# Audio tower on one core: z turned beside pv, tokenizer units that end at halves of a cycle, and q and k projected behind the experts' first products

## What is computed

```python
h = tok(x)                                        # x: 16 x 512 x 128
h = h + attn(layernorm(h))
h = h + ffn(layernorm(h))

# tok: for patches of 8, 16, 32 rows with half a patch as stride
y = einsum('bnk,dk->bnd', patches, W) + b + pos + scale_emb[i]   # 127 + 63 + 31 = 221 rows a batch
# attn: 8 heads of 16, 221 x 221 scores
attn = softmax(q @ k.T / sqrt(16)); out = (attn @ v) @ w_agg.T + b_agg
# ffn: the first 1024 tokens, 8 experts, each token goes to 2 of them
h1 = gelu(xg @ w1[e]); y = h1 @ w2[e]; out[token] += weight * y
```

## Time and profile before

| | us |
|---|---|
| median of 3 timed runs | 293.25 |
| lowest, highest | 283.29, 294.13 |
| the profiled execution | 283.87 |
| its span, first to last instruction | 281.8 |
| TensorE busy in it | 244.3 |
| VectorE, ScalarE, GpSimd busy | 191.2, 140.2, 124.8 |
| mean granted clock of TensorE | 0.973 |

### The profile page before, as it was taken

The page is one execution under the profiler, slowest core; times in us unless marked ns, Lnnn a source line. Parts: engine busy times, 40 slices in busy tenths (PEclk is TensorE's granted clock), DMA queues, the critical chain, the costliest instruction groups (busy, mean ns, idle before and its releaser), DMA issues.

```text
span 281.8 us, 6982 instructions
## 1 busy us (share of the span) xinstructions
PE 244.3 (87%) x2711; PEld 202.4 (72%) x2711; DVE 191.2 (68%) x420; ACT 140.2 (50%) x220; POOL 124.8 (44%) x177
## 2 busy tenths in 40 slices
PE   8999986997997879998896598989898989897894
PEld 8799776765675667776666486868686868685673
DVE  2994765857687758697855337676767676758644
ACT  4860310633323142524355256767676767676460
POOL 6000120111236345647474144868686858664421
PEclk9999999898899999999999689999999999999998
DMA  6999030305437282743332312626363625343422
GB/s 220 416 386 464 9 87 11 87 12 125 139 72 218 50 220 57 206 121 96 89 85 63 73 37 45 127 48 124 50 123 51 125 48 114 49 92 44 101 19 41
DMA packets 29903, 32.00 MB, mean 114 GB/s; under 512 B 3798, under 2 KB 26150, under 8 KB 29840
## 3 DMA queue, kind: packets, MB, share of 16 engines
q1 hardware_dynamic: 25374, 28.39, 35.5%
q0 software_dynamic: 4080, 2.59, 7.2%
q10 hardware_dynamic: 418, 0.58, 0.6%
HBM read 16.24 MB, written 5.95 MB: 79 GB/s over the span
## 4 chain that ended last, share of the span: by engine, by line
PE 66%; DVE 18%; ACT 5%; issue 4%; DMA 3%; SPq 1%; POOL 1%; DVEq 0%; POOLq 0%; ACTq 0%
PE s_ps L1268 13%; PE e_ps L1194 13%; DVE nmax L968 10%; PE e_ps L1462 8%; PE s_ps L1194 8%; PE m_ps L1253 4%; PE m_ps L1447 4%; ACT probs L663 3%; PE e_ps L1447 3%; DMA x_raw<-x 2%; PE m_ps L1410 2%; ACT hidT L715 1%; PE m_ps L1259 1%; PE m_ps L1381 1%; PE m_ps L1260 1%
## 5 line engine op out<-in xcount | busy, mean ns | idle before, releaser
L968 DVE TENSOR_REDUCE nmax<-s_ps 104x4 fp32r<-104x884 f32 (+1 forms) x60 | 61.9, 1073 | 29.2 <-PE s_ps L1268 29.1
L663 ACT ACTIVATE probs<-s_ps 104x888 f32<-104x888 f32 (+1 forms) x60 | 51.3, 907 | 40.3 <-PE s_ps L1268 39.8
L562 POOL DMA_INDIRECT out<-y_sb,idx_u x23 | 36.4, 1582 | 39.6 <-DMA out<-y_sb,idx_u 20.8
L1268 PE MATMUL s_ps<-pair_a 32*104 32x222 f32 (+1 forms) x504 | 34.9, 311 | 15.1 <-DVE nmax L968 10.0
L1268 PEld LDWEIGHTS s_ps<-pair_a 32*104 32x104 f32 (+1 forms) x504 | 21.3, 172 | 30.7 <-DVE nmax L968 15.7
L500 POOL TENSOR_TENSOR var_eps<-mv,eps_t 128x2 f32<-128x2 f32 x16 | 7.0, 437 | 66.4 <-DVE mv L933 66.3
L533 POOL DMA_INDIRECT z_slots<-z,slot_u x20 | 21.3, 1067 | 20.4 <-PE s_ps L1268 16.3
L1462 PE MATMUL e_ps<-w_now,hidT 128*128 128x128 f32 x184 | 25.6, 292 | 2.8 <-DVE zsT L1070 2.7
L1462 PEld LDWEIGHTS e_ps<-w_now,hidT 128*128 128x128 f32 x184 | 23.4, 204 | 4.3 <-issue 4.0
L1381 PE MATMUL m_ps<-probs,v_aug 104*32 104x221 f32 (+1 forms) x480 | 25.8, 353 | 0.0
L1194 PE MATMUL e_ps<-x_hi,w_hi 128*128 128x248 f32 (+3 forms) x88 | 20.1, 361 | 4.4 <-DVE hT L825 4.4
(11 more groups left out here) (163 smaller groups left out, 515.5 us busy)
## 6 DMA issues: line engine op xcount, KB each, us to landing
pair_a<-qk SPq DMA_DIRECT2D x64, 111.0 KB
w_sb<-w SPq DMA_DIRECT2D x8, 512.0 KB
pair_b<-qk SPq DMA_DIRECT2D x32, 111.0 KB
w_raw<-wt SPq DMA_DIRECT2D x6, 512.0 KB, 9.8
x_raw<-x SPq DMA_DIRECT2D x6, 512.0 KB, 10.3
z_slots<-z SPq DMA_DIRECT2D x1, 1518.0 KB, 14.3
zs<-z_slots SPq DMA_DIRECT2D x7, 198.0 KB
x_raw<-x SPq DMA_DIRECT2D x4, 256.0 KB, 5.7
```

Source lines behind the costliest of these rows:

```text
L562: g.indirect_dma_start(rows, bass.IndirectOffsetOnAxis(ap=idx_u[:, at:at + 1], axis=0), y_sb[:, n % 2, i, :], None, compute_op=ALU.add).th ...
L663: s.activation(probs[0:n, blk, 2 * f:2 * f + 2].rearrange("p t u n -> p t (u n)"), s_ps[0:n, 2 * f:2 * f + 2, 0:2 * NE], ACT.Exp, scale=DH ...
L968: v.tensor_reduce(nmax[0:n, blk, 2 * f:2 * f + 2, MAX_ROW[0]:MAX_ROW[1] + 1:2], src, AX_X, ALU.max, negate=True).then_inc(max_ready, 1)
L1268: mm = pe.matmul(dst[0:n, i, u * NE:(u + 1) * NE], a[rs, u, N0 * blk:N0 * blk + n], b[rs, u, :], start=start, stop=stop)
```

## The change

- A row of PLAN has six numbers: p0 is new and stands between pv(c-1) and s1(c,1); p1 and p2 now stand on the two sides of place_max, both behind h_turn. The first half is p0 + p1 + p2. All pm are 0, so nothing stands between place_max and s2(c,0).
- z_turn(c+1) stands behind s1(c,0) and ahead of pv(c-1); it was z_turn(c+2) at the end of the cycle before.
- From cycle 8 on, project_qk stands behind hidden(n,2), qk_high behind GELU 2 and qk_low behind take_max.
- From cycle 7 on, h_turn stands behind s2(c,0), and VectorE evacuates zsT before it copies h. hT_evac at the first half's end stands right behind take_max, ahead of turn.
- lo_x(8) and lo_x(9) stand one cycle earlier.
- load_zs(1) stands ahead of place_qk(8).

```diff
-PLAN = {-2: (3, 11, 0, 0, 0), -1: (4, 6, 0, 16, 20), 0: (4, 8, 0, 6, 10), 1: (2, 6, 2, 5, 6), 2: (3, 7, 2, 4, 6),
...
+PLAN = {-2: (0, 3, 11, 0, 0, 0), -1: (0, 4, 6, 0, 12, 12), 0: (16, 8, 0, 0, 7, 8), 1: (0, 5, 4, 0, 9, 6), 2: (0, 5, 5, 0, 9, 5),
...
@@ SP
+                if n == 0:
+                    load_zs(1)
                 if c + 1 < BATCH:
                     place_qk(c + 1)
...
-                if n == 0:
-                    load_zs(1)
@@ ScalarE
                 gelu(n, 1)
+                gelu(n, 2)
                 if n > 0:
                     qk_high(c + 1)
-                gelu(n, 2)
@@ VectorE
-                    qk_low(c + 1)
+                    if n <= 0:
+                        qk_low(c + 1)
                     if c >= 0:
                         take_max(c)
+                    if n > 0:
+                        qk_low(c + 1)
+                if (c, 0) in UNIT_ENDS:
+                    hT_evac(UNIT_ENDS[(c, 0)])
                 if n >= 0:
+                    zsT_evac(n + 1)
                     if c + 2 < BATCH:
                         late_h_copy(c + 2)
-                    zsT_evac(n + 1)
-                    if c + 2 < BATCH:
                         ln_stats(c + 2)
                 if c - 1 >= 0:
                     turn(c - 1)
...
-                if (c, 0) in UNIT_ENDS:
-                    hT_evac(UNIT_ENDS[(c, 0)])
...
+                if c == 0:
+                    lo_x(8)
                 if c == 1:
-                    lo_x(8)
-                if c == 2:
                     lo_x(9)
@@ TensorE
                 if here:
                     s1(c, 0)
+                if ahead1:
+                    z_turn(c + 1)
                 if behind:
                     pv(c - 1)
+                tok_some(p0)
                 if here:
                     s1(c, 1)
-                tok_some(p1)
                 if n == 0:
                     zs_turn(0)
-                else:
-                    hidden(n, 1)
-                if ahead1:
+                if ahead1 and n <= 0:
                     project_qk(c + 1)
                 if n == 0:
                     hidden(n, 0)
-                    hidden(n, 1)
+                hidden(n, 1)
                 hidden(n, 2)
+                if ahead1 and n > 0:
+                    project_qk(c + 1)
                 if ahead2 and n < 0:
                     h_turn(c + 2)
-                tok_some(p2)
+                tok_some(p1)
                 if here:
                     place_max(c)
+                tok_some(p2)
                 if n >= 0:
                     zs_turn(n + 1)
-                if ahead2 and n >= 0:
-                    h_turn(c + 2)
                 tok_some(pm)
                 if here:
                     s2(c, 0)
+                if ahead2 and n >= 0:
+                    h_turn(c + 2)
                 tok_some(p3)
...
-                if ahead2:
-                    z_turn(c + 2)
```

More of the change, by code:

```diff
@@ L90 @@
 UNIT_AT = {0: 0, 1: 127, 2: 190}
-PLAN = {-2: (3, 11, 0, 0, 0), -1: (4, 6, 0, 16, 20), 0: (4, 8, 0, 6, 10), 1: (2, 6, 2, 5, 6), 2: (3, 7, 2, 4, 6),
-        3: (4, 9, 4, 8, 8), 4: (4, 10, 4, 8, 14), 5: (4, 8, 4, 8, 12), 6: (2, 5, 2, 5, 10)}
+PLAN = {-2: (0, 3, 11, 0, 0, 0), -1: (0, 4, 6, 0, 12, 12), 0: (16, 8, 0, 0, 7, 8), 1: (0, 5, 4, 0, 9, 6), 2: (0, 5, 5, 0, 9, 5),
+        3: (0, 4, 5, 0, 16, 10), 4: (0, 8, 8, 0, 14, 6), 5: (0, 8, 8, 0, 12, 6), 6: (0, 5, 4, 0, 9, 6)}
 PLACES = 6
@@ L143, in unit_ends @@
         for half in range(2):
-            much = sum(PLAN[c][2:] if half else PLAN[c][:2])
+            much = sum(PLAN[c][3:] if half else PLAN[c][:3])
             for s in LEFT[at:at + much]:
@@ L1522, in _ @@
                 here, ahead1, ahead2, behind = 0 <= c < BATCH, 0 <= c + 1 < BATCH, c + 2 < BATCH, c - 1 >= 0
-                p1, p2, pm, p3, p4 = PLAN.get(c, (0, 0, 0, 0, 0))
+                p0, p1, p2, pm, p3, p4 = PLAN.get(c, (0, 0, 0, 0, 0, 0))
                 if here:
                     s1(c, 0)
+                if ahead1:
+                    z_turn(c + 1)
                 if behind:
                     pv(c - 1)
+                tok_some(p0)
                 if here:
                     s1(c, 1)
-                tok_some(p1)
                 if n == 0:
                     zs_turn(0)
-                else:
-                    hidden(n, 1)
-                if ahead1:
+                if ahead1 and n <= 0:
                     project_qk(c + 1)
```

## The result

| | before, forecast | after, measured |
|---|---|---|
| median of the timed runs | 288.27 (now 4 runs), forecast 263.0 | 266.22 (4 runs) |
| lowest, highest | 283.15, 294.13, forecast range 256 to 273 | 265.65, 275.62 |
| profiled execution, its span | 283.87, 281.8 | 265.65, 263.8 |
| mean granted clock in it | 0.973 | 0.997 |

The changed kernel takes 0.939 of the time before (95% interval 0.937 to 0.942), so it is 6.1% faster. This ratio sets the lower runs against each other (283.15 and 283.29 before; 265.65, 266.19 and 266.24 after), while the higher ones (293.25, 294.13; 275.62) are left out of it, though not out of the medians.

The account below looks back on a forecast made before the run. TensorE, busy for 87% of the span, bounds the kernel: its list plus the waits in it. 283.87 less 13.3 (cycles -1 to 6), 7.2 (cycle 7) and 1.0 (later cycles) gives 262.4, taken as 263; range 256 to 273.

Parts of the forecast that it names:

- Cycle 7: Read of zs for round 1 goes ahead of batch 8's q and k copies: 7.2 us gained, between 3 and 8.
- rival 3: Cycle 7: zs is still late, its read waiting for something else; no gain there, 270 us; chance 0.04.
- Cycles -1 to 6: z turned beside pv, halves ending units, tokens moved: 13.3 us gained, s1(7,0) at 131.6 instead of 144.9.
- 3.4 us for the low clock: Cycles 0 to 6: time lost to a granted clock of 0.97 over 100.5 us, part of an 18.2 bound.
- Rival 1: Cycles 0 to 6 give half, 6.5 instead of 13.3, as DVE's list and exponentials replace waits; 269.5 us; chance 0.14.
- the two waits of 1.84 and 1.83: Cycles 1 and 3: pm products ahead of s2(c,0) wait for hT's evacuation; to go with pm at 0.
- its wait of 2.17: Cycle 0: TensorE stands 2.17 us between the halves of s1; z_turn(1) and 16 token products fill it.
- Cycles 8 to 13: Reordered cycles with experts: net 0.15 us a cycle, seven times, 1.0 us gained, between -3 and +3.
- rival 4: Cycles 8 to 13: q and k copies issued 0.9 us later make it slower than before; 290 us; chance 0.02.
- Its nearest row: Landing time of q and k copies judged by zs: 2.78 us issue to use, 2.3 without the issue.
- Rival 2: Runs sit in the high state: clock falls in three to five more places, 1.7 us each; 272 us; chance 0.15.
- up to 10 us above the sum: Whole kernel: a run of the new kernel may still exceed the summed forecast by up to 10 us.

Follow-up runs that it names:

- the repeat: The changed kernel run and profiled once more with nothing altered: 264.54 us, ratio 0.934 to the kernel before.
- the kernel with GpSimd's swap: Changed kernel; in cycles up to 5 GpSimd takes the experts' layernorm powers ahead of the scatter at the cycle's end: 265.33 us, ratio 0.937.
- q and k put back and o_T first: Changed kernel with q and k's old place restored, and o_T (turn, norm) made before VectorE copies h: 261.53 us, ratio 0.924.

## Why the prediction was right, and where its terms were off

**Cycle 7: forecast 7.2, measured 7.3** (22.77 to 15.46), and 6.5 to 7.4 by taking the read alone in and out. The mechanism is the predicted one to the row: issue as soon as the numbers are there, TensorE at it 2.6 us later without a wait, ScalarE's table load last, and s2(7,1) 11.7 us after the cycle's start as forecast. (TensorE ran dry at 157.96 - 5.15 = 152.8 in the earlier trace rows, not at the 152.6 of the forecast, so even the wait of 0.2 that it left had no ground.) That the store of h1 ahead in the queue would hold it (rival 3) is refuted.

**Cycles -1 to 6: forecast 13.3, measured 11.6 in the repeat, 10.2 in the first profile.** s1(7,0) came at 133.3 and 134.7, not at 131.6. The forecast lengths were 13.0, 12.9, 13.6, 12.7, 11.7, 11.6, 12.7; the repeat has 12.74, 13.16, 13.82, 12.92, 12.1, 12.1, 13.14. The start is right (43.3 for 43.4), the first four cycles are within 0.3 each, cycles 4 to 6 are each 0.4 to 0.5 too long. The steps that were sized too small can be named for cycle 4, whose working the forecast shows. Its terms add up to 11.6 (it wrote 11.7), and 12.10 was measured. Cycle 4 of the repeat:

```profile
95.98 0.36 PE L1270 MATMUL s_ps<-pair_a 32*104 32x222 f32 x4
...
99.43 1.01 PE L1255 MATMUL m_ps<-zT,wqkv_sb 128*128 128x221 f32 x4
...
101.67 0.43 PE L1355 MATMUL m_ps<-ident_r,nmax 104*128 104x104 f32 x2
101.94 1.14 PE L1196 MATMUL e_ps<-x_hi,w_lo 128*128 128x248 f32 x8
103.01 0.46 PE L1270 MATMUL s_ps<-pair_a 32*104 32x222 f32 x8
...
103.61 1.86 PE L1196 MATMUL e_ps<-x_hi,w_lo 128*128 128x248 f32 x14
103.73 1.71 ACT L663 ACTIVATE probs<-s_ps 104x888 f32<-104x888 f32 x2 [2.45 <-PE s_ps L1270]
105.49 0.47 PE L1270 MATMUL s_ps<-pair_a 32*117 32x222 f32 x8
...
106.11 0.47 PE L1412 MATMUL m_ps<-wagg_sb,o_T 128*104 128x128 f32 x2
...
108.08 0.35 PE L1270 MATMUL s_ps<-pair_a 32*104 32x222 f32 x4 [0.17 <-ACT probs L663]
```

The first step, 95.98 to 99.43, is 3.45 us, exactly as forecast. Then, forecast and measured, by starts:

| step | forecast | measured |
|---|---|---|
| maxima, to place_max | 2.15 | 2.24 |
| place_max | 0.22 | 0.27 |
| p2, 8 products | 0.92 | 1.07 |
| s2(4,0) | 0.60 | 0.60 |
| p3, 14 products, and exponentials beside them | 1.80 | 1.88 |
| s2(4,1) | 0.65 | 0.62 |
| exponentials, to s1(5,0) | 1.80 | 1.97 |

The excess of 0.5 us has no single cause. 0.25 of it is the exponentials, which the forecast priced at 1.75 to 1.8 from the end of the scores. Those of half 0 end at 103.73 + 1.71 = 105.44, and s2(4,1) starts at 105.49; in cycle 5, with 12 products there instead of 14, the same step is 1.89, so the products do not set it. The last step is 1.97 in cycle 5 too. A further 0.15 is the 8 products of p2, and 0.14 lies in maxima and place_max.

The price of one product was right. In these rows of the trace, and in those of the kernel before, single products of 248 columns start 0.11 to 0.12 us apart, as the forecast's 0.115 has it. What it left out is the end of a run, where 128-row weights give way to the 32-row weights of the scores: the last product of the 8 starts 0.21 us ahead of the first score, and so does the last of the four ahead of s2(4,0) in the kernel before. Ahead of z_turn, whose weights are 104 rows high, this step is 0.12 there:

```profile
116.73 1.84 PE L1194 MATMUL e_ps<-x_hi,w_lo 128*128 128x248 f32 x14
118.41 0.25 PE L1242 MATMUL m_ps<-c_sb,z_sb 104*128 104x104 f32 x1
```

14 products take 118.41 - 116.73 = 1.68 us here, 0.12 each, and the 8 of p2 take 0.134 each. For cycles 5 and 6 the forecast gives no steps, so which of theirs were short is open. There is some luck in the sum as well: cycle 0 came 0.26 shorter than forecast, which hid a third of the 0.7 that cycles 1 to 3 came longer. The forecast's 3.4 us for the low clock was rough: 0.97 of 100.5 makes 3.0.

Rival 1 (half of 13.3 comes) is not what happened, but the repeat lies a quarter of the way to it. That the waits themselves were rightly named is shown for pm, by the kernel before without it: 3.9 us in cycles 1 and 3, where the two waits of 1.84 and 1.83 stood (0.18 each in after, under the 0.3 that the forecast set as a sign). It is shown for x_lo by the 1.5 us of cycle 2, though the whole time did not fall with it. For the p0 products and z_turn between the halves of cycle 0 it is only read off: cycle 0 is 1.8 us shorter, and its wait of 2.17 isn't in the list of after.

**Cycles 8 to 13: forecast 0.15 a cycle, measured 0.12** (14.09 to 13.97). The parts too: z_turn 0.2 (forecast 0.19), and the reordering a loss of 0.07 (forecast 0.2 gained at down, 0.25 lost at o_T). What the forecast did not draw from it is that its own terms made the reordering worthless: undoing it gives 263.3 us. In one cycle with experts of each of the two profiles of after, q's and k's copies came too late, as rival 4 had it. This is the start of cycle 10 of after:

```profile
178.68 0.35 PE L1270 MATMUL s_ps<-pair_a 32*104 32x222 f32 x4 [0.45 <-DMA pair_b<-qk]
```

One cycle pays 0.2 to 0.5 us for it. Rival 4 had the right mechanism, at 0.5 us or less of the 21 that it needed. Its nearest row, 2.3 us from the end of the issue to use, was short for this cycle: the last copy was issued from 174.14 and let TensorE go on at 178.63. By starts, the net of cycles 8 to 13 is 0.2 us in the first profile (84.41 to 84.24) and 0.4 in the repeat, not the 0.9 that six times 0.15 makes.

**The sum.** For the repeat, from its span: 281.8 - 262.3 = 19.5 us, of which the start and cycles 0 to 6 give 11.6, cycle 7 7.4, the rest 0.5. Forecast were 13.3, 7.2, 1.0. The first profile has 1.4 us less, from cycles 4 to 6. There TensorE and VectorE stood still with no cause in the profile (three waits of TensorE for "issue", 2.2 us); what held them is open. So of the 3.2 us between the forecast's 263 and the first measurement (266.22) half is gone in the repeat of the same program (264.54).

**Rival 2**, the clock falling in three to five more places at 1.7 us each, is not what the traces show. The two profiles of after hold no slow stretch before the last 1.4 us of the span. Two relatives have a single long one instead, as the last section shows; the forecast's "up to 10 us above the sum" has the right size, and its cause, more slow stretches in the first cycles, is not theirs.

## What to carry to other kernels

Look at the queues of DMA issues first: a read that stood ready behind issues which waited held TensorE up for 5.15 us here, and one moved line is worth over a third of the gain. When a reordering only trades one wait for another on the same chain, build it by itself. Here the list of waits got shorter and the cycle longer, and asking what the new wait (o_T) stood behind gave 3 us more. Price a run of products by the starts, from its first product to the first one behind it: that takes in its two ends, which count times price leaves out (0.15 us in the 8 products here). Then check what runs beside it: with 14 or with 12 products the step lasted the same.

## What the hardware showed that was not expected

Two profiles hold one slow stretch of over 20 us at the end of the program: the kernel with GpSimd's swap (272.73 in its profiled run, 264.0 to 265.6 in the others) and the one with q and k put back and o_T first (269.99, others 261.5 to 261.9). Windows of the first, then of the changed kernel's repeat (columns as in rows 3):

```profile
230.00:244.00 14.00, 11.99 (x152) 9.49 (x152) 8.34 (x16) 10.87 (x19) 6.60 (x6) 1.00 0.45 87
245.00:265.00 20.00, 20.00 (x162) 14.64 (x164) 6.33 (x10) 4.77 (x7) 4.66 (x3) 0.50 0.13 16
```

```profile
230.00:244.00 14.00, 11.97 (x152) 9.47 (x152) 8.35 (x16) 10.91 (x19) 6.59 (x6) 1.00 0.47 88
244.00:258.00 14.00, 13.23 (x176) 10.03 (x176) 8.25 (x18) 4.92 (x8) 4.66 (x3) 1.00 0.19 24
```

Up to 244 the two are alike to 0.02 us. Then TensorE waits for pair_b in both (in the first its clock falls at 244.4, within that wait), and goes on at half its clock in the one and at full clock in the other. The first products behind that wait, again in this order:

```profile
244.75 0.51 PE L1270 MATMUL s_ps<-pair_a 32*104 32x222 f32 x2 [1.17 <-DMA pair_b<-qk]
```

```profile
244.65 0.35 PE L1270 MATMUL s_ps<-pair_a 32*104 32x222 f32 x2 [1.10 <-DMA pair_b<-qk]
```

In the second profile with such a stretch there is no wait for pair_b at all. Its clock falls at 239.1, inside these scores:

```profile
238.78 0.50 PE L1269 MATMUL s_ps<-pair_a 32*117 32x222 f32 x8 [0.72 <-ACT probs L663]
```

The kernel with q and k put back alone has nearly the same three waits there (0.34, 0.63 and 0.73 against 0.33, 0.64 and 0.72) and keeps its clock. In the first of the two TensorE is busy without a break for 20 us while its clock stays at the 1.2 GHz level; it is back at 1.00 at 264.9, and in the other at 263.0. In the middle of the program a slow stretch ended by itself after some 6 us, also with TensorE busy throughout. The Trainium skill (TensorE: Matmul & The Clock Gate, What's actually happening) has activity release the throttled state; the stretch in cycle 7 agrees, and at the end of the program 20.00 us busy of 20.00 went by at 0.50 before the clock came back. Nearly equal idle times go either way (1.17 and 1.10; 0.72 and 0.73; 1.83 in both profiles of cycle 3), so in this program an idle time of 0.7 to 2 us is a risk and not a price. What tells the cases apart is open. Whether the 10 us between the lowest and the highest run of the kernel before are such a stretch is not shown either: their granted clock is 0.930 in two runs at 292 us and 0.973 to 0.982 in five at 282 to 285, and none of the two has a profile here.
